# A decoder kernel on one core: scatters without a marker and paced, two tiles' turns moved, the causal mask in half the columns

## The chip, the cores and the metric

The kernel runs on one NeuronCore of a Trainium2 chip. The core has TensorE (PE, matrix products), VectorE (DVE), ScalarE (ACT), GpSimd (POOL) and SyncE (SP, which here only issues DMAs), each with its own instruction stream; they meet through semaphores. The metric is device microseconds of one execution. The kernel before takes 493.74 us, the median of three runs (493.35 to 494.02). A separate execution was profiled; its span is 506.3 us.

## The reference

x is 8 sequences of 256 tokens of 128 numbers, ctx the same shape. Three residual layers follow each other, each behind a layer norm:

```
x = x + attn(layernorm(x))          # RMS norm, 16 heads of 64, causal softmax, gate per head, 1024 -> 128
x = x + retention(layernorm(x), ctx, ctx)   # 16 heads of 8, rotary positions, decay mask, no softmax
x = x + moe(layernorm(x))           # 12 experts, top 3 of them, 128 -> 512 -> gelu -> 128
```

In the attention, `sim = where(triu(k=1), -max, q k^T / 8)`, so scores above the diagonal must not count. In the third layer each token goes to the three experts with the largest gate logits, and the three results are added with softmax weights. All data is float32.

## The kernel before, in words

**Attention and retention, per sequence.** b counts the 8 sequences and s the 8 head pairs of one. A step (b, s) is, on TensorE: `scores(b, s)`, the products for q and k of the next pair (`qk_of`), the transposes of the probabilities of the pair before (`turn`), and their product with v (`weigh`). VectorE takes the row maxima, ScalarE the exponentials, and both copy operands. The retention, routing and dispatch of sequence b - 1 run between the steps of sequence b; GpSimd makes the outer products of keys and values (L517, 128x1024), rotates the queries (L493 to L498) and sends rows to the experts (`send`, L553). Sequence 0 stands alone, sequences 1 to 6 are one hardware loop whose turns take the same time each, and sequence 7 stands alone again.

**The causal mask.** `scores` first writes a bias into PSUM (L898): a 0/-3e38 triangle, needed once for each of the two 128x128 diagonal blocks. It is made as a product of an identity (128 rows, bf16) with the triangle, split by its contraction into two halves of 64 rows (n = 0, 1), for each of the two heads (h = 0, 1). Head h uses partitions h*64 to h*64+63, so that both heads' products lie in different row halves of the array. Each of the four products has 256 columns. The products of q and k (L904) are then added on top.

**The third layer in tiles.** Tokens are scattered to a DRAM table with a region per expert (`tokens_by_expert`), 6 indirect DMAs of 128 rows per sequence. 35 tiles follow: tile 0 to 23 of 256 tokens, 24 to 34 of 128 tokens. Tiles 0 to 9 and 24 to 34 are computed in plain float32, tiles 10 to 23 in split products (three matmuls each). The order of the tiles is planned on VectorE in four parts: tiles 0 to 6 can start when 6 sequences are dispatched (EARLY = 7), 7 to 9 when 7 are, and from tile 10 (NEXT = 10) all 8 must be. A tile is: SP loads its rows into `xg` (6 buffers, DEPTH); `turn_tokens` transposes them on TensorE (L1098, into `sc`); ScalarE copies the weights (L805) and the transposed tokens (L810, `tokens_high`); VectorE makes the low parts for split tiles (L1608, L1623, in `tokens`) and copies row numbers and weights (L1630, L1631), for which the scatter of six tiles before must have landed; `up` (L1114 plain, L861 split); ScalarE's gelu (L788); `down` (L1144); VectorE's `results` (L1639, L1642); and `scatter` on GpSimd: one indirect DMA per 128 rows (L620) into `results_by_token`. In the end SP reads that table back (L434), VectorE adds (L1712) and SP stores.

**Order around the change.** Each engine's order is written out by hand. TensorE's is `turn_tokens(n + 1)`, `up(n)`, `down(n - 1)`, except where tile n + 1 is 7 or 10 (`fresh`): there the turn comes after `down(n - 1)`. ScalarE does `up_high` and `tokens_high` of tile n + 1 before the gelu of n, but behind it for the fresh ones; VectorE does `tokens(n + 1)` before `results(n - 1)`, but behind it for the fresh ones. GpSimd's `carry` (L540) is a product of one column (the marker) on which the waits stand; in `scatter` it waits for `f_y` (result ready) and for the marker before. `f_up` counts finished halves of `up`, two per tile.

## Time and profile before

| what | us |
|---|---|
| time, median of 3 runs | 493.74 |
| lowest and highest run | 493.35, 494.02 |
| profiled execution, first to last instruction | 506.3 |
| TensorE busy in it | 447.9 (88%) |
| VectorE, ScalarE, GpSimd busy | 368.6, 334.0, 255.7 |

The times of the table's first two rows are of runs without a profile. The profiled execution is one execution more, 12.6 us longer than the median; no other time is known of it than its span. Instructions are listed by the line of the kernel that issues them, tiles by their names without numbers, and "x16" counts the instructions merged in a row. "Idle before <- X" says how long the engine had nothing to run and which instruction ended that. "remote" and "another core or an unknown queue" mean that the profile shows nothing that ended the wait.

### The profile page before, as it was taken

How to read it: one execution, taken by the hardware profiler on the slowest of the kernel's cores; microseconds unless marked ns; L12 is line 12 of the kernel's file. 1: busy time of each engine (PE TensorE's matmuls, PEld its weight loads, DVE VectorE, ACT ScalarE, POOL GpSimd, SP SyncE). 2: the span in 40 equal slices, each digit the busy share in tenths (PEclk: the TensorE clock that was granted, in tenths of full speed). 3: DMA queues.
4: the chain of work that ended last, by engine and by line, in shares of the span. 5: the costliest groups of instructions: out<-in, count | busy, mean ns of one | idle time of the engine just before them, and what ended most of it. 6: DMA issues, size and time to landing. Idle time of an engine off the chain costs nothing.

```text
span 506.3 us, 12394 instructions
## 1 busy us (share of the span) xinstructions
PE 447.9 (88%) x3628; PEld 375.8 (74%) x3628; DVE 368.6 (73%) x1221; ACT 334.0 (66%) x1037; POOL 255.7 (50%) x398
## 2 busy tenths in 40 slices
PE   1989999999999999999999999767878289999880
PEld 1777787887887887887888788546567279999780
DVE  4765578797897898788889789886876237665456
ACT  3579876876868867878687686444563356775550
POOL 4500025358268267366555735761827534676661
PEclk9999999999999999999999999879999599999995
DMA  8990000000000000000000004982011312222149
GB/s 257 368 260 2 1 2 2 1 26 11 5 16 21 5 16 16 11 10 21 11 0 26 16 1 123 188 122 65 30 46 50 85 36 72 68 60 67 46 112 225
DMA packets 43876, 31.67 MB, mean 63 GB/s; under 512 B 3795, under 2 KB 40071, under 8 KB 43840
## 3 DMA queue, kind: packets, MB, share of 16 engines
q1 hardware_dynamic: 39936, 24.22, 19.5%
q0 software_dynamic: 3472, 6.49, 4.1%
q10 hardware_dynamic: 432, 0.53, 0.3%
q8 instruction: 16, 0.26, 0.2%
q14 instruction: 20, 0.16, 0.1%
HBM read 18.91 MB, written 13.04 MB: 63 GB/s over the span
## 4 chain that ended last, share of the span: by engine, by line
PE 55%; POOL 13%; DVE 10%; issue 10%; another core or an unknown queue 3%; ACT 3%; DMA 3%; SPq 2%; DVEq 0%; ACTq 0%; POOLq 0%
PE zb L861 8%; PE ob L933 6%; PE sc L904 5%; PE zb L1144 4%; PE xb L1007 4%; PE ob L1144 4%; POOL kv L517 3%; PE sc L898 3%; POOL tokens_by_expert L553 3%; PE tb_a L917 3%; PE tb_b L917 2%; PE xb L982 2%; POOL kq L495 2%; PE sc L861 2%
## 5 line engine op out<-in xcount | busy, mean ns | idle before, releaser
L540 POOL TENSOR_TENSOR spare_p<-tri 128x1 f32<-128x1 f32 x71 | 15.8, 222 | 128.4 <-DVE xn L1350 62.9
L686 ACT ACTIVATE qk<-zb 128x512 f32<-128x512 f32 x64 | 38.1, 595 | 53.4 <-PE zb L861 52.6
L620 POOL DMA_INDIRECT results_by_token<-y_sb,row_i x59 | 60.0, 1017 | 22.5 <-issue 22.2
L693 ACT ACTIVATE p_sb<-sc,nmx 128x128 f32<-128x128 f32 x128 | 47.6, 372 | 22.4 <-DVE nmx L1266 22.2
L695 ACT ACTIVATE p_sb<-sc,nmx 128x256 f32<-128x256 f32 x128 | 61.7, 482 | 0.0
L933 PE MATMUL ob<-pT,v_sb 128*64 128x256 f32 (+1 forms) x512 | 57.1, 345 | 0.4 <-DVE oT L1284 0.4
L904 PE MATMUL sc<-qk 64*128 64x256 f32 (+1 forms) x512 | 56.1, 335 | 0.1
L553 POOL DMA_INDIRECT tokens_by_expert<-packed,slot_i x48 | 47.9, 997 | 9.2 <-issue 7.9
L904 PEld LDWEIGHTS sc<-qk 64*128 64x128 f32 x512 | 47.2, 194 | 3.9 <-ACT qk L686 0.6
L1279 DVE TENSOR_TENSOR rg<-rr,gate 128x256 f32<-128x256 f32 x64 | 45.6, 712 | 2.2
L933 PEld LDWEIGHTS ob<-pT,v_sb 128*64 128x64 f32 x512 | 31.7, 138 | 19.7 <-issue 9.3
L1284 DVE TENSOR_TENSOR oT<-ob,pT 128x256 f32<-128x256 f32 x64 | 27.0, 421 | 26.3 <-PE ob L933 26.0
L1266 DVE TENSOR_REDUCE nmx<-sc 128x2 f32<-128x512 f32 x64 | 43.5, 679 | 0.0
L788 ACT ACTIVATE hT<-sc,bup_sb 128x256 f32<-128x256 f32 (+1 forms) x72 | 26.1, 440 | 24.9 <-remote 13.7
L702 ACT ACTIVATE pT<-tb_a 128x512 f32<-128x512 f32 x64 | 39.4, 616 | 3.5 <-PE tb_b L922 3.5
L702 ACT ACTIVATE pT<-tb_b 128x512 f32<-128x512 f32 x64 | 39.9, 623 | 0.0
L861 PE MATMUL zb<-xT_hi,wqk_hi 128*128 128x256 f32 x112 | 36.5, 326 | 0.0
L917 PE MATMUL tb_a<-ident,p_sb 128*128 128x128 f32 x192 | 32.3, 277 | 2.0 <-ACT pT L702 2.0
L1144 PE MATMUL zb<-wdn_all,hT 128*128 x248 | 30.9, 276 | 3.2 <-ACT hT L788 2.9
L1144 PEld LDWEIGHTS zb<-wdn_all,hT 128*128 128x128 f32 x248 | 29.3, 192 | 4.2 <-issue 4.0
L861 PE MATMUL zb<-xT_hi,wqk_lo 128*128 128x256 f32 x112 | 32.0, 286 | 0.0
L917 PE MATMUL tb_b<-ident,p_sb 128*128 128x128 f32 x192 | 31.8, 275 | 0.0
(308 smaller groups left out, 1330.5 us busy)
## 6 DMA issues: line engine op xcount, KB each, us to landing
tokens_by_expert<-padding SPq DMA_DIRECT2D x12, 390.0 KB
xg<-tokens_by_expert SPq DMA_DIRECT2D x24, 130.0 KB
wup_all<-in_L_ffn_Wup SPq DMA_DIRECT2D x1, 3072.0 KB, 15.2
wdn_all<-in_L_ffn_Wdown SPq DMA_DIRECT2D x12, 256.0 KB, 5.3
wkv_sb<-in_L_attn_Wkv SPq DMA_DIRECT2D x2, 512.0 KB, 6.4
ctx_b<-in_ctx SPq DMA_DIRECT2D x8, 128.0 KB
out<-x_all SPq DMA_DIRECT2D x4, 256.0 KB, 3.6
results_by_token<-y_sb,row_i POOLq DMA_INDIRECT x59
```

The costliest lines, as they stand in the source:

```text
L553: pool.indirect_dma_start(out=xs, out_offset=bass.IndirectOffsetOnAxis(ap=slot_i[:, t, k:k + 1], axis=0), in_=packed[:, t, k, :], in_offse ...
L620: pool.indirect_dma_start(out=ys, out_offset=bass.IndirectOffsetOnAxis(ap=row_i[:, u, a:a + 1], axis=0), in_=y_sb[:, u, a, :], in_offset=None,
L693: act.activation(p_sb[:, w, h, 0:P], sc[:, k, S:S + P], ACT.Exp, bias=nmx[:, w, 0, n:n + 1], accum_out=total[:, w, 0, h:h + 1])
L695: act.activation(p_sb[:, w, h, P:3 * P], sc[:, k, 0:S], ACT.Exp, bias=nmx[:, w, 1, n:n + 1], accum_out=total[:, w, 1, h:h + 1]).then_inc(a ...
L702: ins = act.activation(pT[:, s % 2, h, :], tb[h][:, :], ACT.Copy)
L861: ins = pe.matmul(o, lhs[l], rhs[m], start=(n == 0), stop=(last and n == 2), skip_group_check=True)
L904: ins = pe.matmul(sc[:, score_bank(w, h), o:o + n], qk[r, 0, t * P:(t + 1) * P], qk[r, 1, 0:n], start=False, stop=(t == 0), skip_group_che ...
L917: pe.transpose(tb[h][:, k * P:(k + 1) * P], p_sb[:, s % 2, h, k * P:(k + 1) * P], ident[:, :])
L933: ins = pe.matmul(ob[h * DH:(h + 1) * DH, t * P:S], v_sb[:, t, 2 * s + h, :], pT[:, s % 2, h, t * S:(2 + t) * P], start=(t == 0), stop=(t ...
L1144: ins = pe.matmul(ffn_out(n)[:, a * D:(a + 1) * D], hT[:, n % 2, k, a * P:(a + 1) * P], wdn_all[:, bass.ds(e, 1), k, :].rearrange("p a d - ...
L1266: dve.tensor_reduce(nmx[:, w, 1, :], sc[:, w:w + 2, 0:S], AX.X, ALU.max, negate=True).then_inc(v_nm, 1)
L1279: dve.tensor_tensor(rg[:, s % 2, :, :].rearrange("p t (h d) -> p t h d", h=2), bc(rr[:, :, :], 3, DH), bc(gate[:, :, 2 * s:2 * s + 2], 3, ...
```

## The change

**Mask.** Instead of splitting the triangle by contraction, its columns are split: for n = 0 and 1 the product now writes columns n*64 to n*64+63 of both diagonal blocks (2 x 64 columns) with 64 rows of contraction. `pick16` holds the two selections of rows and `mask16` the two half triangles; GpSimd builds them for partitions 0 to 63 and VectorE copies them to 64 to 127. There are still four products per pair, each with 128 columns where it had 256.

**Scatters.** `scatter` has no marker and no `p_cell` semaphore; the first DMA waits for `f_y` itself. Scatters 2 to 7 also wait until `up` of tile n + 4 is finished, 8 to 13 until that of n + 3 is. Scatters 14 to 34 wait for `f_y` alone.

**Last sequence's sends.** `pack` of sequence 7 comes before scatter 1, and the six sends go in pairs: the second pair waits for `up(4)`, the third for `up(5)`.

**Tiles 7 and 10.** `fresh` is gone on all three engines.

```diff
@@ -448,17 +446,23 @@
-            pool.memset(ident16[:, :], 0.0).then_inc(p_chain, 1)
-            pool.memset(mask16[:, :, :], 0.0).then_inc(p_chain, 1)
+            pool.memset(pick16[0:DH, :, :], 0.0).then_inc(p_chain, 1)
+            pool.memset(mask16[0:DH, :, :, :], 0.0).then_inc(p_chain, 1)
...
-            pool.affine_select(out=ident16[:, :], in_=ident16[:, :], compare_op=ALU.not_equal, fill=1.0, base=0,
-                               pattern=[[-1, P]], channel_multiplier=1).then_inc(consts, 1)
-
-            pool.affine_select(out=mask16[:, :, :], in_=mask16[:, :, :], compare_op=ALU.is_ge, fill=NEG, base=0,
-                               pattern=[[0, 2], [-1, P]], channel_multiplier=1).then_inc(consts, 1)
+
+            for n, start in ((0, 0), (1, DH - 1)):
+                pool.affine_select(out=pick16[0:DH, n, :], in_=pick16[0:DH, n, :], compare_op=ALU.not_equal, fill=1.0, base=start,
+                                   pattern=[[-1, P]], channel_multiplier=1).then_inc(p_chain, 1)
+            pool.wait_ge(p_chain, 8)
+            pool.affine_select(out=pick16[0:DH, 1, :], in_=pick16[0:DH, 1, :], compare_op=ALU.is_ge, fill=1.0, base=-DH,
+                               pattern=[[1, P]], channel_multiplier=DH).then_inc(consts, 1)
+
+            for n in range(2):
+                pool.affine_select(out=mask16[0:DH, n, :, :], in_=mask16[0:DH, n, :, :], compare_op=ALU.is_ge, fill=NEG, base=-n,
+                                   pattern=[[0, 2], [-1, DH]], channel_multiplier=1).then_inc(consts, 1)
...
+            def ups_ahead(n):
+
+                ahead = 4 if n < 8 else 3
+                return 2 * (n + ahead + 1)
+
             def scatter(n):
                 u = n % DEPTH
-                pool.wait_ge(p_cell, n + 1)
                 pool.wait_ge(f_y, n + 1)
-                carry(3).then_inc(p_cell, 1)
+                if 2 <= n < 14:
+                    pool.wait_ge(f_up, ups_ahead(n))
...
             send(B - 2, 5)
+            pack(B - 1)
             scatter(1)
-            pack(B - 1)
-            dispatch(B - 1)
+            begin(B - 1)
+            for n in range(T * TOPK):
+                if n in (2, 4):
+                    pool.wait_ge(f_up, 2 * (n // 2 + 4))
+                send(B - 1, n)
...
@@ -817,12 +825,6 @@
-                if n + 1 in (EARLY, NEXT):
-
-                    gelu(n)
-                    up_high(n + 1)
-                    tokens_high(n + 1)
-                    return
                 if n + 1 < TILES:
                     up_high(n + 1)
                     tokens_high(n + 1)
@@ -886,17 +888,16 @@
-                        own, mask = (ident16, mask16) if h == n else (ident16x, mask16x)
                         r = slice(h * DH, (h + 1) * DH)
-                        pe.matmul(sc[:, score_bank(w, h), P:P + S].rearrange("p (a j) -> p a j", a=2), own[r, :],
-                                  mask[r, :, :], start=(n == 0), stop=False, skip_group_check=True)
+                        pe.matmul(sc[:, score_bank(w, h), P:P + S].rearrange("p (a j) -> p a j", a=2)[:, :, n * DH:(n + 1) * DH],
+                                  pick16[r, n, :], mask16[r, n, :, :], start=(n == 0), stop=False, skip_group_check=True)
@@ -1169,14 +1170,11 @@
             for n in range(LAST_CHAIN, TILES):
-                fresh = n + 1 in (EARLY, NEXT)
-                if n + 1 < TILES and not fresh:
+                if n + 1 < TILES:
                     turn_tokens(n + 1)
                 up(n)
                 if n > LAST_CHAIN:
                     down(n - 1)
-                if fresh:
-                    turn_tokens(n + 1)
@@ -1189,13 +1187,9 @@
-            dve.wait_ge(consts, 3)
-            LEFT, RIGHT = slice(0, DH), slice(DH, P)
-            for a, z in ((LEFT, RIGHT), (RIGHT, LEFT)):
-
-                dve.tensor_copy(ident16x[a, :], ident16[z, :])
-                ins = dve.tensor_copy(mask16x[a, :, :], mask16[z, :, :])
-            ins.then_inc(consts_v, 1)
+            dve.wait_ge(consts, 4)
+            dve.tensor_copy(pick16[DH:P, :, :], pick16[0:DH, :, :])
+            dve.tensor_copy(mask16[DH:P, :, :, :], mask16[0:DH, :, :, :]).then_inc(consts_v, 1)
@@ -1683,17 +1677,13 @@
             for n in range(LAST_CHAIN + 1, TILES):
-                fresh = n + 1 in (EARLY, NEXT)
-                if fresh:
-                    results(n - 1)
                 if n + 1 < TILES:
                     tokens(n + 1)
...
-                if not fresh:
-                    results(n - 1)
+                results(n - 1)
```

TensorE's order around tile 7, before (L1098 is a turn, L1114 an `up`, L1144 a `down`; ld_e1 is the load of tile 7, ld_e2 of tile 8):

```order
L1114 MATMUL sc<-xgT_full,wq_sb 128x256 [waits f_gelu,f_hi,f_w]
L1114 MATMUL sc<-xgT_full,wq_sb 128x256 x3
...
L1144 ISA [waits f_y,f_gelu]
L1144 MATMUL zb<-wdn_all,hT 128x128 x2
...
L1098 MATMUL sc<-ident,xg 128x128 [waits f_hi,ld_e1]
L1098 MATMUL sc<-ident,xg 128x128
L1098 MATMUL sc<-ident,xg 128x128 [waits f_hi,ld_e2]
```

and now (L1099, L1115 and L1145 are the same three):

```order
L1099 MATMUL sc<-ident,xg 128x128 [waits f_hi,ld_e1]
L1099 MATMUL sc<-ident,xg 128x128
L1115 MATMUL sc<-xgT_full,wq_sb 128x256 [waits f_gelu,f_hi,f_w]
L1115 MATMUL sc<-xgT_full,wq_sb 128x256 x3
...
L1145 ISA [waits f_y,f_gelu]
L1145 MATMUL zb<-wdn_all,hT 128x128 x2
...
L1099 MATMUL sc<-ident,xg 128x128 [waits f_hi,ld_e2]
```

The turn of tile 7 has moved ahead of `up(6)` and `down(5)`; at tile 10 (ld_e4) the same happens with `up(9)` and `down(8)`.

VectorE's order around tile 10, before (L1639 and L1642 are `results`, L1608 and L1623 the low parts, L1630 the row numbers; the rows left out are register loads, the copy of the weights and two small steps of a plan):

```order
L1639 TENSOR_TENSOR y_sb<-ob,bdn_sb 128x256
L1642 TENSOR_SCALAR y_sb<-y_sb,weight 128x128 [waits v_chain]
L1642 TENSOR_SCALAR y_sb<-y_sb,weight 128x128
L1608 TENSOR_TENSOR xgT_lo<-sc,xgT_hi 128x256 [waits f_hi]
...
L1623 TENSOR_TENSOR wup_lo<-wup_all,wup_hi 128x512
L1630 COPY row_i<-xg 128x2 [waits scattered4]
```

and now:

```order
L1602 TENSOR_TENSOR xgT_lo<-sc,xgT_hi 128x256 [waits f_hi]
...
L1617 TENSOR_TENSOR wup_lo<-wup_all,wup_hi 128x512
L1624 COPY row_i<-xg 128x2 [waits scattered4]
...
L1633 TENSOR_TENSOR y_sb<-ob,bdn_sb 128x256
L1636 TENSOR_SCALAR y_sb<-y_sb,weight 128x128 [waits v_chain]
L1636 TENSOR_SCALAR y_sb<-y_sb,weight 128x128
```

The low parts of tile 10 no longer stand behind the results of tile 8.

GpSimd's order from the last sequence's pack on, before:

```order
L540 TENSOR_TENSOR spare_p<-tri 128x1 [waits f_y,p_cell]
L620 DMA results_by_token<-y_sb,row_i 6144x128 x2
L540 TENSOR_TENSOR spare_p<-tri 128x1 [waits dispatched,v_xn3]
L548 COPY packed<-xn 128x3x128 x2
L540 TENSOR_TENSOR spare_p<-tri 128x1 [waits p_pack,v_slot]
L553 DMA tokens_by_expert<-packed,slot_i 27904x130 x6
L540 TENSOR_TENSOR spare_p<-tri 128x1 [waits f_y,p_cell]
L620 DMA results_by_token<-y_sb,row_i 6144x128 x2
```

and now:

```order
L544 TENSOR_TENSOR spare_p<-tri 128x1 [waits dispatched,v_xn3]
L552 COPY packed<-xn 128x3x128 x2
L624 DMA results_by_token<-y_sb,row_i 6144x128 [waits f_y]
L624 DMA results_by_token<-y_sb,row_i 6144x128
L544 TENSOR_TENSOR spare_p<-tri 128x1 [waits p_pack,v_slot]
L557 DMA tokens_by_expert<-packed,slot_i 27904x130 x2
L557 DMA tokens_by_expert<-packed,slot_i 27904x130 [waits f_up]
L557 DMA tokens_by_expert<-packed,slot_i 27904x130
L557 DMA tokens_by_expert<-packed,slot_i 27904x130 [waits f_up]
L557 DMA tokens_by_expert<-packed,slot_i 27904x130
L624 DMA results_by_token<-y_sb,row_i 6144x128 [waits f_up,f_y]
L624 DMA results_by_token<-y_sb,row_i 6144x128
```

Scatter 1 has moved behind the pack, the marker is gone from the scatters, and waits for TensorE's `up` stand between the DMAs.

## Rows read from the trace of the kernel before

**Rows 1.** The page's busy times, and its slices of TensorE, its clock and GpSimd.

```profile
PE 447.9 (88%) x3628; PEld 375.8 (74%) x3628; DVE 368.6 (73%) x1221; ACT 334.0 (66%) x1037; POOL 255.7 (50%) x398
...
PE   1989999999999999999999999767878289999880
...
PEclk9999999999999999999999999879999599999995
```

**Rows 2.** One turn of the loop: busy us of each engine (instructions), granted clock.

```profile
178.50:219.05 40.55, 40.50 (x348) 32.82 (x347) 34.20 (x109) 31.25 (x104) 23.33 (x37) 1.00 0.04 13
```

**Rows 3.** TensorE in time order: a mask group, and twelve-column products.

```profile
183.03 0.28 PE L898 MATMUL sc<-mask,ident 64*128 64x256 bf16 x1
...
183.26 0.82 PE L904 MATMUL sc<-qk 64*128 64x256 f32 x8
...
376.40 0.17 PE L1031 MATMUL xb<-hit,ones 128*128 128x12 bf16 x1
376.43 0.17 PE L1032 MATMUL xb<-hit,tri 128*128 128x12 bf16 x1
```

**Rows 4.** The chain that ended last, pieces of one loop turn: start, us, what.

```profile
181.32 3.87 POOL kv L517 x2
...
196.62 0.92 POOL qt L498
...
197.64 0.70 DVE prod L1332
...
198.38 0.73 PE xb L1007 x2
```

**Rows 5.** VectorE in time order, same turn: one product twice.

```profile
183.24 2.23 DVE L1279 TENSOR_TENSOR rg<-rr,gate 128x256 f32<-128x256 f32 x1
...
191.50 0.43 DVE L1279 TENSOR_TENSOR rg<-rr,gate 128x256 f32<-128x256 f32 x1
```

**Rows 6.** TensorE around tiles 7 and 10, in time order.

```profile
401.61 0.66 PE L1098 MATMUL sc<-ident,xg 128*128 128x128 f32 x2 [11.15 <-ACT xgT_full L810]
402.06 1.91 PE L1114 MATMUL tb_a<-xgT_full,wq_sb 128*128 128x256 f32 x4
...
411.59 1.03 PE L1114 MATMUL tb_a<-xgT_full,wq_sb 128*128 128x256 f32 x4
...
417.58 0.41 PE L1098 MATMUL sc<-ident,xg 128*128 128x128 f32 x2 [2.09 <-DVE wup_lo L1623]
...
473.51 1.15 PE L1144 MATMUL zb<-wdn_all,hT 128*128 x8 [1.34 <-ACT hT L788]
```

**Rows 7.** ScalarE, then, in time order: the gelu of tile 6 and what follows.

```profile
396.93 0.84 ACT L788 ACTIVATE hT<-sc,bup_sb 128x256 f32<-128x256 f32 x2 [11.63 <-remote]
399.80 0.84 ACT L788 ACTIVATE hT<-sc,bup_sb 128x256 f32<-128x256 f32 x2 [2.03 <-remote]
...
401.10 0.37 ACT L810 ACTIVATE xgT_full<-sc 128x256 f32<-128x256 f32 x1
```

**Rows 8.** GpSimd in time order: the last send, scatter 2, and a scatter near the end.

```profile
388.90 0.97 POOL L553 DMA_INDIRECT tokens_by_expert<-packed,slot_i  x1 [0.30 <-issue]
...
390.25 1.02 POOL L620 DMA_INDIRECT results_by_token<-y_sb,row_i  x1 [0.16 <-issue]
...
478.83 0.18 POOL L540 TENSOR_TENSOR spare_p<-tri 128x1 f32<-128x1 f32 x1 [0.53 <-DVE y_sb L1642]
479.53 0.99 POOL L620 DMA_INDIRECT results_by_token<-y_sb,row_i  x1 [0.52 <-issue]
```

**Rows 9.** The chain later on: two split tiles, then the last scatters.

```profile
447.49 1.79 PE zb L1144 x16
...
454.36 1.79 PE zb L1144 x16
...
481.43 2.90 DMA results_by_token<-y_sb,row_i
```

**Rows 10.** VectorE in time order, the same split tiles: a copy of row numbers.

```profile
451.77 0.17 DVE L1630 COPY row_i<-xg 128x2 int32<-128x2 int32 x1
```

More of the change, by code:

```diff
@@ L114, in decoder @@
         ident = sb("ident", [P, P])
-        ident16 = sb("ident16", [P, P], BF16)
-        mask16 = sb("mask16", [P, 2, P], BF16)
-        ident16x = sb("ident16x", [P, P], BF16)
-        mask16x = sb("mask16x", [P, 2, P], BF16)
+        pick16 = sb("pick16", [P, 2, P], BF16)
+        mask16 = sb("mask16", [P, 2, 2, DH], BF16)
         tri = sb("tri", [P, P])
@@ L321, in decoder @@
         v_var, a_log, a_guess = sem("v_var"), sem("a_log"), sem("a_guess")
-        p_kv, p_q, p_sum, p_ret, p_pack, p_keep, p_cell, p_chain = (
-            sem(n) for n in ("p_kv", "p_q", "p_sum", "p_ret", "p_pack", "p_keep", "p_cell", "p_chain"))
+        p_kv, p_q, p_sum, p_ret, p_pack, p_keep, p_chain = (
+            sem(n) for n in ("p_kv", "p_q", "p_sum", "p_ret", "p_pack", "p_keep", "p_chain"))
         pe_CNT, v_hit, v_filled, v_slot, v_pad, v_first, v_next, v_plan, v_fin = (sem(n) for n in ("pe_CNT", "v_hit", "v_filled", "v_slot", "v_pad", "v_first", "v_next", "v_plan", "v_fin"))
@@ L480, in _ @@
             pool.dma_start(xs[E * CAP:ROWS, :].rearrange("(a p) w -> p a w", p=P), padding[:, 0:SLOTS // P, :]).then_inc(dispatched, 16)
-            pool.memset(spare_p[:, :], 0.0).then_inc(p_cell, 1)
+            pool.memset(spare_p[:, :], 0.0)
             pool.wait_ge(ld_tab, 16)
@@ L484, in _ @@
             LINKS = 3 + 1 + 3
-            BASE = 6
+            BASE = 8
             def rotate(b, link0, src, dst, which):
@@ L562, in begin @@
                 carry(1)
-            def dispatch(b):
-                begin(b)
-                for n in range(T * TOPK):
-                    send(b, n)
             def keep(b):
@@ L766, in _ @@
                     act.activation(bup_sb[:, :, :].rearrange("p e c -> p (e c)"), xb[:, 0:E * HC], ACT.Copy).then_inc(a_bup, 1)
-                    act.wait_ge(consts, 5)
+                    act.wait_ge(consts, 6)
                     act.wait_ge(consts_v, 1)
@@ L888, in scores @@
                 if b == 0 and s == 0:
-                    pe.wait_ge(consts, 5)
+                    pe.wait_ge(consts, 6)
                     pe.wait_ge(consts_v, 5)
```

## The prediction

> **What bounds the kernel now.** I read the busy times and the slices first. TensorE is busy 88% of the span and no other engine above 73%; its digits are 9 and 8 over the first half, fall to 6 and 7 in the slices from 354 to 405 us, and come back to 9 [rows 1]. So the first 350 us are near full and what can be gained by filling lies in the third layer. In the slices around 390 the granted clock reads 5: the half level.
>
> Second, one turn of the loop, which holds one of sequences 1 to 6: 40.55 us, with TensorE busy 40.50 of them at clock 1.00 [rows 2]. That looks bound by TensorE alone. The chain of waits says otherwise for half of the turn. From 178.0 to 198.4 it runs over GpSimd (packs, kv, sends, query rotation), a VectorE product and only then to TensorE's L1007 at 198.38 [rows 4]; from there to the turn's end it is on TensorE. VectorE is held in it too: a product that takes 0.43 us took 2.23 and ended at 185.47, beside GpSimd's kv, which ended at 185.19 [rows 4, 5]. TensorE is as good as full there, yet if its own work shrank, L1007 would still come when VectorE's product is ready.
>
> Third, the third layer on TensorE. Two breaks stand out: 11.15 us ahead of the turn of tile 7, which ended with ScalarE's copy of transposed tokens, and 2.09 us before the first turn behind tile 10's, which ended with VectorE's low part [rows 6]. ScalarE had waited 11.63 and 2.03 us for something the profile does not show [rows 7], while GpSimd issued DMA after DMA (six sends, then scatters 2 to 4, 0.3 us apart) [rows 8]. The engine then came back at half clock: the same four products took 1.91 us at 402.06 and 1.03 at 411.59 [rows 6]. Counted together: 10.5 of the 11.15 are this stall (0.6 is the ordinary break, below); from 401.6 to the end of the slice with the 5, at 405.1, TensorE ran at half level and lost half of it, 1.8; and at 473.51 it had waited once more for ScalarE's gelu, 1.3 [rows 1, 6]. That is 13.6 us, and 506.3 - 13.6 = 492.7, below the median of 493.74. So, if a span and a time measure the same, the timed runs held about 1 us of these stalls and the other 12.6 belong to the profiled execution alone.
>
> **The change part by part.**
>
> *Mask.* A group's first product starts at 183.03 and the first score product at 183.26, so four products of 256 columns cost 0.23 us, because those of the two heads run side by side [rows 3]. With half the columns the streaming halves: 0.107 to 0.115 us saved per group. There are 8 sequences of 8 groups, 64: at most 64 x 0.115 = 7.4 us. What could keep it from halving is the price of loading weights, which are still loaded four times; products of 12 columns with weights of their own start 0.03 us apart [rows 3], so no such price shows above 0.03. How many groups lie on the path? In a loop turn 4 of 8 come between 178.0 and 198.4, where GpSimd sets the time, and their gain ends as a wait in front of L1007; 4 come behind it. Six turns give 24 groups. Sequence 0 has no retention beside it, and sequence 7 is mixed with the early tiles; I count 8 of their 16. 32 x 0.107 = 3.4 us, between 0 (each group's time lost to the next wait) and 7.4.
>
> The rows give 0.03 us as spacing of small products with their own weights. The Trainium skill (TensorE: Matmul & The Clock Gate, Back-to-back issue gap) says that a stream of weight loads and products of 128 columns is held at about 81 ns each by both together, well over the 56 ns of the columns alone. By that four products, two by two, would shrink from 0.23 to 0.16 and not to 0.12, and the sum would be some 1.2 us smaller; this trace shows no floor of that kind in its smallest products.
>
> *Tile 7.* Today its turn stands behind down(5), ScalarE copies it behind a gelu, and the next turn needs that copy. Outside the stall this costs the copy, 0.37 us, and 0.14 from its end at 401.47 to the turn at 401.61 [rows 6, 7], and about as much on the way to ScalarE: 0.6 us. In the new order turn and copies lie under up(6) and down(5). Gain 0.6, between 0 and 1. The load of tile 7 must be there a step earlier; it was issued long before.
>
> *Tile 10.* The same, and worse, for a split tile: VectorE's results of tile 8 stand ahead of the low parts. The break is 2.09 us [rows 6]. In the new order the low parts lie under up(9) and down(8), as with all split tiles, whose period holds no such break: 6.87 us for two [rows 9]. Gain 2.1. What could be late next is the load of tile 10, which needs the plan of all sequences; the turn now comes a step of about 4 us earlier, and its load was in the profiled execution in time by more than that. Without the stall the last sends set it, and they finish about 1 us sooner because scatter 1 stands behind the pack. Bounds 0.5 and 2.4.
>
> *Marker.* GpSimd's own time in the third layer is no bound: TensorE sets the period. Only behind the last tile is the marker on the path: result ready, marker at 478.83 for 0.18, 0.52 of idle, DMA at 479.53 [rows 8]. From the marker's start to the DMA are 0.70; a DMA behind a DMA starts after 0.30 [rows 8]. So up to 0.57 could go; the first DMA now waits itself and has its own start cost. I take 0.4, between 0 and 0.57.
>
> *Waits for up.* Behind each of these waits stand all later DMAs of GpSimd, and for them waits VectorE at L1630 (the row numbers of tile n + 6). For split tiles scatter(n) may begin when up(n + 3) is done, for tiles 2 to 7 at up(n + 4). Take the later: up ends at 447.49 [rows 9]. Two DMAs take 1.0 + 0.3 + 1.0 us [rows 8] and the landing behind the last ones up to 2.90 [rows 9], so all has landed 4 to 5.2 us after up(n + 4). VectorE copies the numbers of tile n + 6 at 451.77 [rows 10], 4.3 us after. The wait is 0 to 0.9 us, and VectorE has about a microsecond idle in each period before the results are due, and the bank that these free is needed only a tile later. So 0. Do the waits remove the stall? In the profiled execution perhaps; for the median I count nothing, as the timed runs held at most a small part. Bounds: 12 us slower and 13.6 faster, both below.
>
> *The start.* GpSimd makes the tables with three more selections and VectorE copies two times instead of four, beside the first loads. 0, within 0.3.
>
> Sum: 3.4 + 0.6 + 2.1 + 0.4 = 6.5 us. On the profiled execution's own time that is 506.3 - 6.5 = 499.8, and 486.2 if its stalls go as well; on the median 493.74 - 6.5 = **487.2 us**.
>
> **The rivals.**
>
> *A: the whole mask gain.* TensorE's 40.50 of 40.55 [rows 2] speaks for it: if GpSimd and VectorE only look critical because they share a pace that TensorE sets, all 64 groups count, 7.0 instead of 3.4. Against it, GpSimd's rows from 181 to 198 hang on each other [rows 4]. 493.74 - 7.0 - 3.1 = 483.6. The Trainium skill (Perfetto Trace Analysis, Identifying the Most-Contended Engine) would start from the engine with the highest occupancy, which is TensorE, and points to this case. Chance 0.12.
>
> *B: the timed runs hold a good part of the stall, and the paced DMAs end it.* The difference of 12.6 us between the profiled execution and the median is one number with two readings. If all of it is extra stall, 13.6 - 12.6 = 1.0 us of stall stays in the median; if all of it is a fixed difference between a span and a time, the median holds all 13.6. Halfway, 7.3 us: 487.2 - 7.3 = 479.9. For it: ScalarE's wait of 11.63 began in a run of back-to-back DMAs [rows 7, 8], and the new order breaks that run into pairs. Against it: the wait's cause isn't in the profile, and pairs may do the same. The Trainium skill (Runtime: NRT & Kernel Launch, The ~15µs preamble/postamble breakdown) states a constant 6.2 us of a profile's total that the reported time leaves out; by an estimate with it 7.2 us of the stall would be in the median. Chance 0.18.
>
> *C: most is hidden.* Only tile 10 and a few mask groups count, 1 to 3.5 us: 490.2 to 492.7, middle 491.5. For it: in a loop turn VectorE and GpSimd have waits of their own behind L1007 as well, which I have not all excluded. Chance 0.17.
>
> *D: slower.* The paced scatters land late. For 12 tiles (2 to 13) VectorE waits at the row numbers; once landing comes over 8 us after up(n + 4), so that the results behind the copy are late for the bank that down(n + 6) needs, each wait goes through to TensorE. With one microsecond per tile that is 12: 487.2 + 12 = 499.2. It decides from landings about 3 us later than the slowest that I saw (2.90 after the issue). Against it: fewer DMAs run together, which makes them land sooner. Chance 0.08.
>
> **How the numbers follow.** My forecast has 0.45, with a range of its own from 484.5 to 489.7; A 0.12, B 0.18, C 0.17, D 0.08. The range that should hold the time 8 times in 10 reaches down into B, where I leave out its lower 40%, and up over most of C, leaving out D: 478.5 to 492.0. Faster by over 0.2% means under 492.75 and slower over 494.73; 0.2% is about what a measurement of this kernel can tell from no change. Forecast, A, B and nearly all of C are faster: 0.88. A remainder of C and of D gives 0.05 for within 0.2%, the rest of D 0.07.
>
> **What would show it.** The loop turn: about 40.1 us if half the mask gain counts, 39.7 if all, 40.5 if none; in the first case a new idle of TensorE of about 0.4 before L1007 with VectorE's product as its end. A mask group of 0.12 us; 0.16 would mean that loading weights holds it. TensorE's 2.09 before the turn behind tile 10 gone, and VectorE's low part ahead of the results of tile 8. ScalarE's waits for something unknown between 380 and 402 gone and the clock at 9 throughout, if pairs of DMAs are harmless; if they stay, the wait's cause is not the unbroken row of DMAs. GpSimd's rows in the third layer without markers, idle ahead of each pair. VectorE's wait at the row numbers under 1 us. I am wrong if the turn is still 40.5, if the load of tile 10 holds the turn of TensorE, or if VectorE's wait at the row numbers is followed by an idle TensorE.

## The result, and the profile after

The changed kernel takes 488.90 us (median of 4 runs, 488.06 to 489.58), the kernel before 493.88 (4 runs, 493.35 to 494.71): ratio 0.9899, 95% interval 0.9869 to 0.9928. That is 5.0 us faster, with 3.6 to 6.5 in the interval; 6.5 were forecast, and the time lies in the forecast's own range. All ratios here compare runs in the fast state only, so they need not be the quotient of the two medians beside them. The profiled execution has a span of 486.8 us, and its time was 488.6, so a span is 1.8 us shorter than a time. With that, the profiled execution of before was near 508: its stalls do not belong to the timed runs, and none of the 33 runs of before that later ran beside the experiments on the first chip took more than 496.1.

The page of the changed kernel, the same rows as [rows 1]:

```profile
PE 444.9 (91%) x3628; PEld 374.2 (77%) x3628; DVE 366.0 (75%) x1219; ACT 335.5 (69%) x1037; POOL 248.3 (51%) x366
...
PE   1889999999999999999999999986987999999980
...
PEclk9999999999999999999999999986798999999995
```

A loop turn and the long middle of the third layer, as busy us of each engine (the order of columns is that of [rows 2]):

```profile
176.50:216.75 40.25, 40.11 (x348) 32.48 (x346) 33.94 (x109) 31.32 (x104) 23.58 (x37) 1.00 0.04 13
378.00:470.00 92.00, 92.00 (x764) 90.39 (x763) 59.63 (x241) 65.57 (x174) 59.01 (x61) 1.00 0.26 71
```

The turn is 0.30 us shorter. From 378 to 470 TensorE is busy without a break, and the clock stays at 1.00. The group of [rows 3] and the score products behind it, on TensorE in time order:

```profile
181.01 0.29 PE L899 MATMUL sc<-mask,pick 64*128 64x128 bf16 x4
181.13 0.87 PE L905 MATMUL sc<-qk 64*128 64x256 f32 x8
181.93 0.39 PE L863 MATMUL zb<-xT_hi,wqk_hi 128*128 128x256 f32 x1
```

Before, the same three stood at 183.03, 183.26 [rows 3] and 184.00. The mask group went from 0.23 to 0.12 us, but the eight score products behind it from 0.74 to 0.80.

Tiles 7 to 11 now turn without a break; TensorE's turns from tile 7 on:

```profile
386.08 0.38 PE L1099 MATMUL sc<-ident,xg 128*128 128x128 f32 x2
389.81 0.38 PE L1099 MATMUL sc<-ident,xg 128*128 128x128 f32 x2
393.54 0.38 PE L1099 MATMUL sc<-ident,xg 128*128 128x128 f32 x2
397.27 0.38 PE L1099 MATMUL sc<-ident,xg 128*128 128x128 f32 x2
401.00 0.38 PE L1099 MATMUL sc<-ident,xg 128*128 128x128 f32 x2
404.45 0.38 PE L1099 MATMUL sc<-ident,xg 128*128 128x128 f32 x2
```

Steps of 3.73 us (3.45 to the last), and no idle in brackets where [rows 6] had 2.09 us. GpSimd's scatters come in pairs, without markers between:

```profile
392.76 0.97 POOL L624 DMA_INDIRECT results_by_token<-y_sb,row_i  x1 [1.44 <-PE tb_b L1115]
394.04 0.97 POOL L624 DMA_INDIRECT results_by_token<-y_sb,row_i  x1 [0.30 <-issue]
...
472.73 0.97 POOL L624 DMA_INDIRECT results_by_token<-y_sb,row_i  x1 [0.90 <-DVE y_sb L1636]
474.00 1.37 POOL L624 DMA_INDIRECT results_by_token<-y_sb,row_i  x1 [0.30 <-issue]
```

The pair at 392.76 waited for an `up` (L1115). The six sends of the last sequence, from 379.74 on, still follow each other 0.30 us apart as in [rows 8]: their two waits for `up` held none of them.

### The profile page after: what moved, and what is told of

Read it like the earlier page. It is cut to its first block, busy times and chain, and to the rows that moved or that the text cites. A ratio compares the mean times of both kernels' runs of the same rounds, so it can differ in the third digit from the quotient of the medians.

```text
span 486.8 us, 12340 instructions
## 1 busy us (share of the span) xinstructions
PE 444.9 (91%) x3628; PEld 374.2 (77%) x3628; DVE 366.0 (75%) x1219; ACT 335.5 (69%) x1037; POOL 248.3 (51%) x366
## 4 chain that ended last, share of the span: by engine, by line
PE 56%; POOL 15%; issue 10%; DVE 10%; ACT 3%; DMA 3%; SPq 2%; POOLq 0%; DVEq 0%; ACTq 0%
PE zb L863 7%; PE ob L934 6%; PE zb L1145 5%; PE sc L905 5%; PE ob L1145 5%; POOL tokens_by_expert L557 4%; POOL kv L521 3%; PE xb L1008 3%; PE tb_a L918 3%; PE tb_b L918 2%; PE xb L983 2%; PE sc L863 2%; PE sc L1115 2%; POOL kq L499 2%; PE tb_a L863 2%
## 5 line engine op out<-in xcount | busy, mean ns | idle before, releaser
L544 POOL TENSOR_TENSOR spare_p<-tri 128x1 f32<-128x1 f32 x36 | 7.3, 202 | 105.3 <-DVE xn L1344 69.2
L905 PE MATMUL sc<-qk 64*128 64x256 f32 (+1 forms) x512 | 59.4, 351 | 0.4 <-ACT qk L694 0.4
L934 PE MATMUL ob<-pT,v_sb 128*64 128x256 f32 (+1 forms) x512 | 58.1, 350 | 0.4 <-DVE oT L1278 0.4
L1278 DVE TENSOR_TENSOR oT<-ob,pT 128x256 f32<-128x256 f32 x64 | 26.9, 421 | 27.3 <-PE ob L934 26.5
L1273 DVE TENSOR_TENSOR rg<-rr,gate 128x256 f32<-128x256 f32 x64 | 36.6, 571 | 2.2
L1145 PE MATMUL zb<-wdn_all,hT 128*128 x248 | 30.7, 275 | 1.5 <-ACT hT L796 1.5
L863 PE MATMUL zb<-xT_lo,wqk_hi 128*128 128x256 f32 x112 | 31.8, 284 | 0.0
```

The costliest lines, as they stand in the source:

```text
L863: ins = pe.matmul(o, lhs[l], rhs[m], start=(n == 0), stop=(last and n == 2), skip_group_check=True)
L905: ins = pe.matmul(sc[:, score_bank(w, h), o:o + n], qk[r, 0, t * P:(t + 1) * P], qk[r, 1, 0:n], start=False, stop=(t == 0), skip_group_che ...
L934: ins = pe.matmul(ob[h * DH:(h + 1) * DH, t * P:S], v_sb[:, t, 2 * s + h, :], pT[:, s % 2, h, t * S:(2 + t) * P], start=(t == 0), stop=(t ...
L1145: ins = pe.matmul(ffn_out(n)[:, a * D:(a + 1) * D], hT[:, n % 2, k, a * P:(a + 1) * P], wdn_all[:, bass.ds(e, 1), k, :].rearrange("p a d - ...
```

## The experiments

**The parts alone.** Four kernels on one chip, each beside the same 33 runs of before (median 493.98 us).

`mask_only`, the kernel before with

```diff
-                        pe.matmul(sc[:, score_bank(w, h), P:P + S]..., own[r, :], mask[r, :, :], ...)
+                        pe.matmul(sc[:, score_bank(w, h), P:P + S]...[:, :, n * DH:(n + 1) * DH], pick16[r, n, :], mask16[r, n, :, :], ...)
```

> The kernel before with the new mask alone. Theory 1: a group of four mask products shrinks by 0.107 us, but the first score product behind it takes 0.054 more, because its float32 weights (0.187 us to load) are no longer covered; net 0.053 per group, of which some five and a half of eight in a loop turn count: the turn falls from 40.55 to 40.25 as in the changed kernel, and the whole by 1.8 (loop) plus about 0.6 (sequences 0 and 7) = 2.4 us, ratio 0.995. Theory 2: the groups' 0.107 all counts and something else in the changed kernel took back the rest: turn 39.7, total -6 us, ratio 0.988. Rival 3: the mask's gain is lost again in sequence 7, where TensorE falls to half clock: ratio 0.998 to 1.

492.53 us, ratio 0.9979 (0.9949 to 1.001). By the timed runs alone it is not told from no change, and 0.9979 is as near to rival 3 as to theory 1. Its trace has the turn of theory 1:

```profile
152.94:193.19 40.25, 40.12 (x347) 32.47 (x345) 33.92 (x108) 31.30 (x104) 23.54 (x37) 1.00 0.04 13
```

Theory 2, with a turn of 39.7, fell. How much sequence 7 varies, which rival 3 builds on, is looked at below, with the clock.

`turns_only`, the kernel before with

```diff
-                fresh = n + 1 in (EARLY, NEXT)
-                if n + 1 < TILES and not fresh:
+                if n + 1 < TILES:
                     turn_tokens(n + 1)
```

and the same on ScalarE and VectorE.

> The kernel before with tiles 7 and 10 turned like the others, nothing else. Theory: 0.6 us at tile 7 and 2.1 at tile 10 go, -2.7 us, ratio 0.9945, and no idle time of TensorE of over 0.3 us before the turn behind tile 10. Rival: the turn of tile 10 now waits for its load (plan and DMA of tile 10), and the gain is 1 us or less, ratio 0.998.

489.35 us, ratio 0.9942 (0.9909 to 0.9975): as the theory has it, and by far the largest part of the result. Its size is known roughly: the interval holds 1.2 to 4.5 us, and the medians are 4.6 apart. What it removes is best read in the trace of `mask_only`, which still has the old order and no stall; TensorE's turns of tiles 7 to 12:

```profile
391.14 0.38 PE L1101 MATMUL sc<-ident,xg 128*128 128x128 f32 x2
392.08 0.41 PE L1101 MATMUL sc<-ident,xg 128*128 128x128 f32 x2 [0.56 <-ACT xgT_full L814]
395.89 0.38 PE L1101 MATMUL sc<-ident,xg 128*128 128x128 f32 x2
403.13 0.38 PE L1101 MATMUL sc<-ident,xg 128*128 128x128 f32 x2
405.57 0.41 PE L1101 MATMUL sc<-ident,xg 128*128 128x128 f32 x2 [2.05 <-DVE wup_lo L1622]
409.15 0.38 PE L1101 MATMUL sc<-ident,xg 128*128 128x128 f32 x2
```

The breaks stand ahead of the turns of tiles 8 and 11, which wait for the copies of tiles 7 and 10: 0.56 and 2.05 us, against 0.6 and 2.1 forecast. From the last product of the last gate logits to the turn of tile 12 it takes 35.13 us there and 31.92 in the changed kernel, 3.2 less, which is 0.6 more than the two breaks. The rest lies beside them: from the turn of tile 6 to that of tile 12, at full clock in both traces, it is 25.26 us (from 383.89) against 22.10 (from 382.35), and around each break the steps lose about 0.3 us more than the idle time shown.

`pool_only`, the kernel before with the new `scatter`, pack and sends.

> The kernel before with the changes on GpSimd alone: no marker, the last sequence's pack ahead of scatter 1, sends and scatters in pairs that wait for up. Theory: -0.4 us behind the last tile, nothing else: ratio 0.999 (0.998 to 1.0), and a profiled execution without the wait of 11 us between 385 and 397. Rival 1: the timed runs of before held part of those waits, ratio 0.985 to 0.995. Rival 2: late landings hold VectorE, ratio 1.002 or more.

493.46 us, ratio 0.9979 (0.9948 to 1.0009): nothing clear of the noise, and the interval leaves hardly any room for either rival. Its profile has none of the unexplained waits, but it doesn't show that the pairs removed them: the profiles of `mask_only` and `turns_only`, in which sends and scatters follow each other 0.16 to 0.31 us apart as in [rows 8], have none either.

`unpaced`, the changed kernel without

```diff
-                if 2 <= n < 14:
-                    pool.wait_ge(f_up, ups_ahead(n))
...
-                if n in (2, 4):
-                    pool.wait_ge(f_up, 2 * (n // 2 + 4))
```

> The changed kernel without the waits for up: the last sequence's sends and scatters 2 to 13 go as soon as their data is ready. Theory: the same time as the changed kernel within 0.5 us (ratio to before 0.990), as GpSimd is bound by the results from tile 14 on anyway; if the profiled execution shows ScalarE's unexplained wait near 385 again, the unbroken row of DMAs goes with it, without costing the timed runs. Rival: the pairs carry several us of the gain, ratio to before 0.995 to 1.01.

488.86 us, ratio 0.9917 (0.9883 to 0.995), the time of the changed kernel. The unexplained waits did not appear, although sends and scatters followed each other 0.30 us apart again. What the pacing does is visible on VectorE, in the waits from 378 to 470 us, first of the changed kernel, then of `unpaced` (waited for, us in total, times, longest):

```profile
DVE row_i L1624 <- DMA results_by_token<-y_sb,row_i: 5.7, 5, 1.8
```

```profile
DVE row_i L1620 <- DMA results_by_token<-y_sb,row_i: 0.2, 1, 0.2
```

With the pacing VectorE waits 5.5 us more, in five places and up to 1.8 us at a time, and TensorE, 92.00 of 92.00 us busy, feels none of it.

**What became of the mask's gain.** Two kernels on another chip, on which before took 508.11 us; their loop turns were compared; their times (507.01 us for `last_wide`, ratio 0.9954 with 0.9903 to 1.0005, and 506.71 for `no_mask`, 1.0014 with 0.9976 to 1.0053) tell nothing apart.

`last_wide`, the changed kernel with the columns split 32 + 96 and the tables as they were, so that it masks other scores than it should:

```diff
-[:, :, n * DH:(n + 1) * DH], pick16[r, n, :], mask16[r, n, :, :]
+[:, :, (0, 32)[n]:(32, P)[n]], pick16[r, n, :],
+    mask16[r, :, :, :].rearrange("p n a j -> p (n a j)")[:, 0:(64, 192)[n]].rearrange("p (a j) -> p a j", a=2)
```

> The changed kernel with the same 128 columns of mask per head split 32 + 96 instead of 64 + 64, the wider product last (the mask is wrong in places; equal work). Theory 1 (cover of the weight load): the group still takes about 0.12 us or a little less, and the score group 0.77 instead of 0.80, since the load of its first weights begins with the last mask product, which is now 0.08 long instead of 0.053; a loop turn 0.1 to 0.2 shorter than 40.25. Rival (the 0.054 has another cause, such as the number of columns before it): score group stays at 0.80 and the turn at 40.25.

The score products take 0.77 us in its trace, TensorE in time order:

```profile
121.78 0.28 PE L899 MATMUL sc<-mask,pick 64*128 64x64 bf16 x4
121.90 0.85 PE L905 MATMUL sc<-qk 64*128 64x256 f32 x8
122.67 0.39 PE L863 MATMUL zb<-xT_hi,wqk_hi 128*128 128x256 f32 x1
```

`no_mask`, the changed kernel with the four mask products left out, so that every token sees all others (the first products of q and k then start the sum in PSUM themselves):

> The changed kernel without any causal mask (its attention also sees later tokens): the four mask products of each group are left out. It shows how much of TensorE's time in a group counts. Theory 1 (the score product behind the group pays 0.054 us for its weights because the short mask products don't cover the load): 0.122 + 0.054 = 0.176 us less per group, the score group is back at 0.74, and in a loop turn some five and a half of eight groups count: 40.25 falls to 39.3. Theory 2 (GpSimd's chain hides half of the turn): 4 groups count, 39.55, and the new idle time stands ahead of L1008. Rival 3 (TensorE alone sets the turn): 8 count, 38.85.

Here the same products take 0.85 us. The third row is a later group, and the last line has the busy times of a whole turn:

```profile
122.74 0.92 PE L901 MATMUL sc<-qk 64*128 64x256 f32 x8
123.60 0.38 PE L863 MATMUL zb<-xT_hi,wqk_hi 128*128 128x256 f32 x1
...
126.78 0.92 PE L901 MATMUL sc<-qk 64*128 64x256 f32 x8 [0.54 <-ACT p_sb L703]
```

```profile
153.25:193.46 40.21, 39.35 (x315) 31.65 (x313) 33.95 (x110) 31.37 (x105) 23.54 (x37) 1.00 0.04 13
```

Put in a row by the length of the last mask product pair (a pair of 256 columns each took 0.107, so 192 take 0.080 and 128 take 0.053):

| last mask products, us | 0.107 (before) | 0.080 (`last_wide`) | 0.053 (changed) | none (`no_mask`) |
|---|---|---|---|---|
| score products, us | 0.748 | 0.775 | 0.802 | 0.853 |

Theory 1 holds for the load: the 0.77 that it forecast for `last_wide` came true. Its turn did not: 40.18 us, the mean of five, is 0.07 shorter than 40.25, where 0.1 to 0.2 was forecast. For `no_mask` it was wrong twice: the score group is not back at 0.74, as nothing else covers that load, and the turn is 40.20 us. TensorE is busy only 39.35 of 40.21 us there and waits for ScalarE's exponentials ahead of two of the eight groups, 0.51 and 0.18 us in the turn shown (0.54 in the row above).

In the other kernels the same two groups wait as well, in the middle of their mask products: the second head's may start only when ScalarE is done with its scores. One of them, before and in the changed kernel:

```profile
208.23 0.28 PE L898 MATMUL sc<-mask,ident 64*128 64x256 bf16 x1
208.49 0.28 PE L898 MATMUL sc<-mask16x,ident16x 64*128 64x256 bf16 x2
...
209.47 0.38 PE L861 MATMUL zb<-xN_hi,wqk_hi 128*128 128x256 f32 x1
```

```profile
205.92 0.60 PE L899 MATMUL sc<-mask,pick 64*128 64x128 bf16 x4
206.33 0.92 PE L905 MATMUL sc<-qk 64*128 64x256 f32 x8
207.18 0.39 PE L863 MATMUL zb<-xN_hi,wqk_hi 128*128 128x256 f32 x1
```

From its first mask product to the product behind its scores this group takes 1.24 us before and 1.26 now, and the other that waits (212.80 and 210.54) 1.04 and 1.01; the remaining six take 0.98 and 0.92. So six groups of eight bring 0.053 us each and two bring nothing in sum, which is the 0.3 us by which the turn is shorter. With both `last_wide` and `no_mask` at 40.2, a turn has a second bound there, in which ScalarE's exponentials have a part, and the changed kernel is within 0.05 us of it.

**The clock.** In the 33 runs of before, time and mean granted clock go together: 6 runs at 0.981 took 489.5 to 490.0 us, 8 at 0.971 took 492.6 to 494.0, 16 at 0.966 to 0.968 took 494.2 to 496.1. Most of this spread can come from one stretch. From the output products of the last loop turn (L982, at 307.45 before) to the first gate logits of sequence 7 (373.63) the traces take, with the time at half level in it:

| trace | stretch, us | at half level, us |
|---|---|---|
| `turns_only` | 65.07 | 6.8 |
| before | 66.17 | 10.2 |
| changed | 67.82 | 17.1 |
| `unpaced` | 68.87 | 13.7 |
| `mask_only` | 68.95 | 17.1 |
| `pool_only` | 69.82 | 17.1 |

In the traces TensorE's clock falls to its half level in sequence 7 after idle times of 2.8 and 4.0 us (VectorE's rg is late there). Two kernels keep TensorE busy in these:

```diff
+                if b == B - 1 and s in (3, 5):
+                    for _ in range(20 if s == 3 else 30):
+                        pe.transpose(tb[0][:, BLOCKS * P:], ident[:, :], ident[:, :])
                 pe.wait_ge(v_rg, at(b, PAIRS, s + 1))
```

`filled_waits` is the changed kernel with this, `filled_three` has 14 more such transposes ahead of the wait for xn3T.

> The changed kernel with idle TensorE kept busy in sequence 7: ahead of its two waits for rg (2.8 and 4.0 us of idle) it makes 20 and 30 transposes of the identity that nobody reads (2.1 and 3.2 us at full clock). Theory: the half clock that follows those waits (3.4 us from 319 and 13.6 from 332 in the changed kernel's profile) goes; each us of it costs 0.76 us of time (fit over 33 runs of before), and the mean granted clock rises from 0.970 to 0.98 or more; 3 to 8 us faster than the changed kernel, ratio to before 0.975 to 0.985. Rival: the half clock is no effect of the idle time, the clock stays at 0.970 and the time too, or 0.5 us worse for the dummies that run over the wait (0.990).

> As filled_waits, and 14 more such transposes ahead of the wait for xn3T of sequence 7 (1.9 us of idle at 370, followed by 3.4 us of half clock in the changed kernel's profile). Theory: that spell goes too and 1 to 2.5 us with it against filled_waits. Rival: what follows there waits for VectorE anyway, no difference beyond 0.5 us.

506.05 us, ratio 0.9983 (0.995 to 1.0016), and 505.24, ratio 0.9964 (0.993 to 0.9999), on the chip with before at 508.11. The changed kernel was not among these, so all was run again, with it and with a fourth kernel, `filled_old_mask_b`: `filled_three` with the mask products of before.

> The changed kernel once more, beside the next three on one chip. On a chip where before takes 494 us: 488.9 (ratio 0.990). Theory: on a chip whose third layer holds long unexplained waits (before at 508) the ratio is nearer to 0.995, since TensorE waits there in the changed kernel as well.

> The changed kernel with the two waits for rg filled with transposes that nobody reads. Theory: the half clock after those waits goes (in its first profile none was left before 338), which takes 1 to 3 us off the changed kernel. Rival: sequence 7 waits for VectorE anyway, so that full clock only lengthens TensorE's waits: under 0.5 us.

> As filled_waits_b, with the wait for xn3T filled too. Theory: 2 to 4 us faster than the changed kernel, mean granted clock 0.98 against 0.970, and a narrower spread of the runs than that of before. Rival: as for the two waits, under 0.5 us beside filled_waits_b.

> filled_three_b with the mask of before (256 columns per product). With the clock steadier, the pair tells what the mask is worth. Theory 1 (net 0.053 us per group, five and a half of eight count in a turn): 2.0 to 2.8 us slower than filled_three_b, loop turn 40.55 against 40.25. Rival (the mask's worth in the changed kernel was luck of the clock): within 0.5 us.

| kernel | median us | ratio to before | mean clock |
|---|---|---|---|
| before | 505.90 (35 runs) | 1 | 0.962 |
| after_again_b | 503.23 | 0.9949 (0.9907 to 0.9991) | 0.965 |
| filled_waits_b | 501.97 | 0.9946 (0.991 to 0.9982) | 0.971 |
| filled_three_b | 501.91 | 0.992 (0.9887 to 0.9953) | 0.979 |
| filled_old_mask_b | 505.20 | 1.0003 (0.9965 to 1.0042) | 0.975 |

The window from 318 to 348 us, first of the changed kernel in its trace of this chip (`after_again_b`), then of `filled_three_b`:

```profile
318.00:348.00 30.00, 24.67 (x154) 17.88 (x155) 22.31 (x68) 15.45 (x51) 13.78 (x21) 0.72 0.87 131
```

```profile
318.00:348.00 30.00, 23.18 (x199) 18.09 (x198) 24.67 (x82) 15.75 (x52) 15.13 (x24) 1.00 0.89 137
```

The clock went from 0.72 to 1.00 and stayed there to the logits: the half level there follows the idle time. But of the 16.8 us at half level (0.28 of 0.5, times 30) little arrives, since VectorE is busy 24.67 of the 30 us in `filled_three_b` and TensorE, apart from the added transposes, waits for it. From the second wait for rg to the logits:

```profile
333.84 0.48 PE L923 MATMUL tb_a<-ident,rg 128*128 128x128 f32 x1 [4.01 <-DVE rg L1273]
...
372.02 0.61 PE L1021 MATMUL xb<-fwg_sb,xn3T 128*128 128x12 f32 x4 [1.85 <-ACT xn3T L841]
```

```profile
333.58 0.33 PE L926 MATMUL tb_a<-ident,rg 128*128 128x128 f32 x1 [0.74 <-DVE rg L1279]
...
370.19 0.61 PE L1027 MATMUL xb<-fwg_sb,xn3T 128*128 128x12 f32 x4 [0.32 <-ACT xn3T L841]
```

38.18 us in the changed kernel, 36.61 in the filled one. Over the whole stretch of the table above it is 67.79 (17.1 at half level) against 65.08 (none), 2.7 us less. The third layer gave it back in these two traces: from the logits to TensorE's last product it took 114.5 us in the changed kernel and 116.2 in the filled one, where ScalarE waited 4.72 us for something unexplained before it copied the tokens of tile 6. In the timed runs the medians differ by 1.3, and the intervals overlap. The theory's size (3 to 8 us at first, then 2 to 4) is not confirmed; the 0.76 us that it took from the 33 runs is the price of a microsecond of clock lost, which is two at half level. Its clock (0.979) and its narrower spread came true: 499.4 to 504.0 us, where before had 501.9 to 511.2. `filled_three_b` has the lowest median of this chip, and that it beats the changed kernel is likely, not shown.

The mask: `filled_old_mask_b` is 3.3 us slower than `filled_three_b`, and the two intervals don't overlap. That is more than the 2.0 to 2.8 expected, and its clock was 0.004 lower as well, so not all of it need be the mask's. Its loop turn is the better witness, at full clock in both: 40.53 us against 40.25, as forecast, 1.7 in six turns. So the mask has a worth of its own, and luck of the clock alone is excluded.

On this chip before took 12 to 14 us more than on the first and the changed kernel 14. In the changed kernel's two traces all of it lies in the third layer: the logits of sequence 7 begin at 372.17 and 372.02. Its waits there, from 375 to 495 us:

```profile
DVE y_sb L1633 <- remote: 13.3, 4, 5.6
ACT xgT_hi L818 <- remote: 6.6, 2, 3.6
ACT xgT_full L818 <- remote: 3.1, 2, 2.3
POOL results_by_token L624 <- remote: 1.8, 1, 1.8
ACT hT L796 <- remote: 1.7, 1, 1.7
```

These are waits like those of [rows 7], with the paced scatters in place. Waits of this kind stand in all eight traces of this chip. The profile of before has them too, 26.7 us in sum, and its time was near 508, which is what before takes on this chip: that profile may come from a chip of this kind. Which chip it was is not known.

## Why the prediction was right, point by point

The faster time and the breaks in the third layer came as forecast; that the total came so near is in part luck, as the mask term had two errors that pull against each other, and the tiles brought more than their term while the marker brought nothing.

- *What bounds the kernel.* The first reading held: TensorE, and the breaks in the third layer. The second failed. I read the chain of waits as if GpSimd set the first half of a turn [rows 4], so that mask time saved there would end as a wait at L1007. The stretch between the mask groups that started at 176.48 and at 199.05, with GpSimd's whole piece of the chain in it, took 22.57 us before and takes 22.34 (174.51 to 196.85) now, about four groups at 0.053, and TensorE has no idle time over 0.3 us ahead of L1008. GpSimd's rows follow TensorE's pace there. Rival A, which said so, was right on the place and wrong on the sum.
- *Mask: 3.4 forecast, 1.8 to 2.0 found.* The group did shrink by the 0.107 us that I took. Against that, more than half of the groups count: six of eight in a loop turn. Half of the groups at twice the worth make 3.4 us, as much as all 64 at the true worth, so the two errors pull against each other; the groups that wait for ScalarE leave the rest. From the first mask group behind the first v products (26.91) to the output products of the last loop turn (307.45) it took 280.54 us before, and 280.35 to 280.42 in the other three traces with the old mask; the changed kernel takes 278.62 (25.74 to 304.36), and `mask_only` 278.54. What sequence 7 adds can't be told from its variation. Ahead of this stretch the clock hides the gain. In the first 25 us the granted clock reads 1.00 in every trace, but products of the same shape (L861, 128x256) take 0.41 us at first and 0.28 later. They become short at about 24 us in the trace of before, at 22 in that of the changed kernel and at 15 in that of `turns_only`. So the first L1007 came at 73.6, 72.0 and 72.4 us. The rule of the Trainium skill (TensorE: Matmul & The Clock Gate, Back-to-back issue gap), that load and product together set the spacing, pointed the right way, though with its 81 ns at the wrong place: the mask group itself reached 0.12, and the cost fell on the group behind.
- *Tiles 7 and 10: 0.6 and 2.1.* Breaks of 0.56 and 2.05 us, gone; 3.2 us in the trace. The break that I placed ahead of the turn of tile 7 stands ahead of that of tile 8: tile 7's own turn was at 390.08. The load of tile 10 was in time.
- *Marker: 0.4 at the end.* It did not reach the end. From the start of the last y_sb to the last scatter's DMA it is 1.08 us (472.92 to 474.00), where it was 1.82 (492.88 to 494.70). But the chain ends over SP's issues and a reading of the results table: the last DMA of the chain, pT<-results_by_token, was issued 3.05 us after the last y_sb's start before (495.93) and 2.57 after (475.49), and took 5.42 us before and 6.44 after. From TensorE's last product to the end it is 14.4 us after and 13.9 before; over the six traces of the table above it is 13.9 to 14.6 with the marker and 13.8 to 15.4 without, so 0.4 us can't be seen there. I had looked only at GpSimd's DMA, and the 0.57 that I gave as the most does not follow from the rows, which give 0.70 - 0.30 = 0.40.
- *Waits for up: 0.* Right. The wait at the row numbers was up to 1.8 us, where I had 0 to 0.9, and was covered all the same.
- *Stall (rival B).* It does not exist in the timed runs of the first chip. My sum of 492.7 for an execution without it was sound: with the 1.8 us between span and time it makes 494.5. The span of 486.2 that I gave for the changed kernel without stalls met a measured 486.8, nearer than its terms deserve.

The sum that the traces leave is 1.9 (mask, up to sequence 7) + 3.2 (tiles) + 0 (scatters) = 5.1 us, against 5.0 measured with an interval of 3.6 to 6.5. Of the timed runs of the parts only `turns_only` is clear of no change, so that the mask's share rests on the traces and on the pair of filled kernels.

## What to carry to other kernels

A product is also the cover under which the weights of the next one are loaded. Before a product is shortened, add its length to that of the group behind it: here, with mask products of up to 0.107 us, their sum didn't change for the last pair. And a chain of waits that runs over another engine is no proof that this engine sets the pace; that TensorE was busy 40.50 of 40.55 us was the better witness.

## What the runs showed of the hardware that I had not expected

- One kernel's time goes with how long the half level lasts. The profile of before had it for 6.8 us from 335 on, that of the changed kernel for 13.6 us from 332.7 on, at idle times of 3.96 and 4.02 us, nearly alike. The 33 runs of before spread from 489.5 to 496.1, so a single run of this kernel tells nothing of 2 us. That the half level makes the spread is shown in part: filling the idle time raised the mean clock from 0.965 to 0.979 and took 2.7 us off sequence 7 in the traces, but only 1.3 off the medians.
- The granted clock reads 1.00 from the start, while the lengths of the same products show that TensorE runs slower up to 15 to 24 us. So the first stretch of a trace is better judged by a product's length than by the clock's row.
- Two chips differ by 14 us (2.9%) with the same program, through waits in the third layer that the profile ascribes to nothing: 26.5 us in sum over the engines in the changed kernel's profile there, none in its first profile or in those of `mask_only`, `turns_only`, `pool_only` and `unpaced`. They come with the pairs of DMAs (on the second chip) and without them (the profile of before), and stay away with and without them on the first. What they wait for stays open.
